# Decoder of two layers: the second layer's chain of the next group woven with the experts of this one

## The reference, cut to what matters

```python
# second layer, x: (16, 100, 256), each part on layernorm(x)
x = x + attn(ln(x))      # q, k, v = bitlinear(h, ternary weights); 16 heads of 16; causal softmax; bitlinear out
x = x + xattn(ln(x))     # q of h (256x256), k and v of the context (128x256), 16 heads, 361 keys, out 256x256
x = x + ffn(ln(x))       # 8 experts and one shared: (gelu(x Wg) * (x Wu)) Wd, weights of the best two of 8

def bitlinear(x, w, g):  # xq: rms norm, then rounded to 8 bits by token; wq: rounded to -1, 0, 1
    return activation_quant(rmsnorm(x, g)) @ weight_quant(w).T
y = einsum('tei,te,eih->th', gelu(g) * u, cw, Wd)    # cw: gate weights, zero for all but two experts
```

## Time and profile before

| | us |
|---|---|
| time, median of 3 runs | 1668.27 (1666.18 to 1669.59) |
| the profiled execution's own time | 1667.32 |
| its span, first to last instruction | 1665.6 |
| PE busy | 1284.8 (77%) |
| DVE busy | 1008.3 (61%) |
| ACT busy | 513.7 |
| POOL busy | 413.2 |
| mean granted clock of PE | 0.861 |

### The profile page before, as it was taken

How to read it: one execution, slowest core, us unless ns; L and a number is a source line. 1 busy time by engine, 2 the same in 40 slices (tenths; PEclk the granted TensorE clock), 3 DMA queues, 4 the chain that set the end, 5 groups by cost and what they waited for, 6 DMA issues and landing times.

```text
span 1665.6 us, 24431 instructions
## 1 busy us (share of the span) xinstructions
PE 1284.8 (77%) x7936; PEld 886.7 (53%) x7936; DVE 1008.3 (61%) x2148; ACT 513.7 (31%) x1269; POOL 413.2 (25%) x528
## 2 busy tenths in 40 slices
PE   2678877878783999952659878689787697986988
PEld 1455644645543566631347654367554575545755
DVE  4457577566563233327668675768657686676852
ACT  2233323324231222201216422246113362233630
POOL 1132234335152100026522112221213212032100
PEclk9688878978896999985769989679898798997998
DMA  9510100390105111111225210144100450104501
GB/s 373 210 47 1 32 16 8 108 382 21 57 18 213 53 45 45 42 39 47 98 45 115 64 40 12 35 90 99 41 12 1 101 122 16 25 11 88 118 7 43
DMA packets 69692, 122.42 MB, mean 73 GB/s; under 512 B 25404, under 2 KB 55100, under 8 KB 68032
## 3 DMA queue, kind: packets, MB, share of 16 engines
q1 hardware_dynamic: 63936, 110.04, 22.0%
q0 software_dynamic: 5632, 10.77, 2.3%
HBM read 67.69 MB, written 53.07 MB: 73 GB/s over the span
## 4 chain that ended last, share of the span: by engine, by line
PE 39%; issue 31%; DVE 10%; POOL 9%; POOLq 3%; DVEq 3%; ACT 2%; DMA 2%; SPq 1%; another core or an unknown queue 0%; ACTq 0%
PE ps L1150 7%; PE ps L1169 3%; PE ps L1323 3%; PE ps L1397 3%; PE ps L1339 3%; PE ps L526 2%; POOL experts L1792 2%; PE ps L1309 2%; PE ps L534 2%; POOL headbd L682 2%; PE ps L1068 1%; PE ps L1046 1%; PE ps L595 1%; PE ps L1410 1%; PE ps L1057 1%
## 5 line engine op out<-in xcount | busy, mean ns | idle before, releaser
L1638 ACT ACTIVATE probs<-ps,small 100x361 f32<-100x361 f32 x256 | 141.5, 558 | 94.9 <-DVE small L2372 89.4
L2372 DVE TENSOR_REDUCE small<-ps 100x2 f32<-100x722 f32 x128 | 115.7, 907 | 37.5 <-PE ps L1309 37.3
L1150 PE MATMUL ps<-every,xT_t 128*128 x256 | 121.7, 599 | 0.4 <-issue 0.4
L1397 PE MATMUL ps<-hT,experts 128*128 128x400 f32 x288 | 115.1, 550 | 1.2 <-DVE small L731 1.2
L1323 PE MATMUL ps<-cst,probs 100*121 100x100 f32 x768 | 104.7, 272 | 7.8 <-DVE probsT L2380 7.4
L1323 PEld LDWEIGHTS ps<-cst,probs 100*121 100x121 f32 x768 | 95.2, 186 | 22.3 <-issue 13.5
L2380 DVE TENSOR_SCALAR probsT<-ps 121x600 f32<-121x600 f32 x128 | 99.2, 775 | 9.8 <-PE ps L1323 9.8
L1339 PE MATMUL ps<-probsT,values_ 121*32 121x100 f32 x1536 | 91.3, 254 | 0.9 <-DVE probsT L2380 0.9
L1309 PE MATMUL ps<-k_stack,q_stack 96*100 96x362 f32 x256 | 82.4, 403 | 6.4 <-ACT probs L1638 5.7
L1199 PE MATMUL ps<-identb,xq 100*128 100x100 bf16 x128 | 13.6, 242 | 88.2 <-DVE y L2247 50.1
L1397 PEld LDWEIGHTS ps<-hT,experts 128*128 128x128 f32 x288 | 59.0, 213 | 41.2 <-issue 12.0
(11 more groups left out here) (328 smaller groups left out, 2896.0 us busy)
## 6 DMA issues: line engine op xcount, KB each, us to landing
k_stack<-key_d SPq DMA_DIRECT2D x192, 90.5 KB, 3.2
tok_d<-wt SPq DMA_DIRECT2D x1, 14848.0 KB, 45.7
res_d<-wt SPq DMA_DIRECT2D x1, 14848.0 KB, 42.8
every<-e_d SPq DMA_DIRECT2D x8, 1536.0 KB, 15.4
ctxT<-ctxT_d SPq DMA_DIRECT2D x8, 726.0 KB, 4.3
key_d<-k_hi SPq DMA_DIRECT2D x32, 181.0 KB, 2.8
key_d<-k_lo SPq DMA_DIRECT2D x32, 181.0 KB, 3.2
gates<-gate_d SPq DMA_DIRECT2D x28, 200.0 KB, 4.4
```

Of the source, the lines that this page charges most:

```text
L1150: ins = e.matmul(ps[:, 2 * i + t % 2, :], xT_t[:, t % 2, c, :], every[:, bass.ds(base + (i * DC + c) * HID0, HID0)], start=(c == 0), stop= ...
L1397: ins = e.matmul(bank(2 * i + j % 2, n=NT), w[:, c, :], hT[:, c, :], start=(c == 0), stop=(c == DC - 1))
L1638: ins = e.activation(f_e[:, n % 2, i, 0:LC], bank(2 * (n % 2) + i, S, LC), ACT.Exp, bias=h_nm[:, n % 2, i:i + 1], accum_out=h_sum[:, b, h: ...
L2372: inc(e.tensor_reduce(h_nm[:, n % 2, 0:2], ps[0:S, 2 * (n % 2):2 * (n % 2) + 2, 0:LC], AX, ALU.max, negate=True), "F_nm")
```

## The change

Self attention of the second layer now takes the code of the first layer's, 16 units of 4 heads. `before_e`, this attention and `after_e` of group g+1 form one chain of 57 steps (18, 21 and 18), and the twelve steps of group g's experts are dealt into it: `dealt` takes an expert step behind the chain's steps 1, 2, 4, 8, 9, 12, 15, 19, 38, 42, 46 and 50. So blocks 0 to 4 and the gate weights lie in `before_e`, block 5 just ahead of the attention, and blocks 6, 7, 8 and the last down and sum in `after_e`.

To have banks for it, the experts use banks 0 to 3 alone: one for gate, one for up (so `gate_up(j)` waits until DVE has read block j-1), two for the sum. `before_e` takes separate banks for its two halves. `after_e` uses one bank for each half. Gate and hidden values and the experts' tokens (`hTG`) lie in weights' space `wt` that is no longer needed. The residual is updated in place in `xall`, and `x_free` is gone. On DVE the first block's product now stands ahead of the gate weights. The loop over groups is unrolled. SP's transfers are the same, but the output of group g is sent from within the feed of group g+1.

```diff
+BEFORE_E, AFTER_E = 9, 9
+GATED_AT = (1, 2, 4, 8, 9, 12, 15, 19, 38, 42, 46, 50)
...
+def both(first, second, rounds):
+    for _ in range(rounds):
+        for st in (first, second):
+            next(st, None)
+            yield
+def dealt(chain, extra, at):
+    for i, _ in enumerate(chain):
+        if i in at:
+            next(extra)
...
@@ PE @@
-            def attend(g, routed):
+            def attend(pre, g, routed=False):
...
             def before_e(g, h):
+                t, o = (6, 4)[h], (7, 5)[h]
...
             def after_e(g, h):
-                yield from toT_pe(e, "E_", g, h, "rTp", b0, xn, ("E_rx", 1))
+                turn_pe(e, "E_", g, h, "rTp", 4 + h, xn, ("E_rx", 1))
+                yield
...
                 if h == 1:
                     e.wait_ge(ld["ctxT3"].sem, g * 16 + 16)
-                    for i in range(3):
-                        kv(g, 0, i)
-                yield
+                    kv(g, 0, 0)
+                yield
+                kv(g, 0, 1 + h)
+                yield
...
+            def inner(g):
+                yield
+                yield
+                yield from attend("E_", g)
+                yield from both(after_e(g, 0), after_e(g, 1), AFTER_E)
+            def chain(g):
+                yield from both(before_e(g, 0), before_e(g, 1), BEFORE_E)
+                yield from inner(g)
...
-            in_turn(late(before_e(0, 1)), before_e(0, 0))
+            in_turn(before_e(0, 0), before_e(0, 1))
+            list(inner(0))
             def group_pe(g, last=False):
-                W(e, "E_kT", g, 1, 1)
-                W(e, "E_v", g, 1, 1)
-                self_pe(e, "E_", g)
-                in_turn(after_e(g, 0), after_e(g, 1))
...
                 if last:
-                    in_turn(experts_g(g))
+                    list(experts_g(g))
                 else:
-                    in_turn(late(before_e(g + 1, 1)), before_e(g + 1, 0), experts_g(g))
+                    dealt(chain(g + 1), experts_g(g), GATED_AT)
+                    W(e, "G_acc", g)
             def experts_g(g):
-                for j in range(E1 + 1):
-                    if j < E1:
-                        if j >= 2:
-                            W(e, "G_hid", g, j - 1)
...
+                def gate_up(j):
+                    if j:
                         W(e, "G_hid", g, j)
+                    for i in range(2):
...
+                            ins = e.matmul(bank(i, n=NT), w[:, c, :], hTG[:, c, :],
+                                           start=(c == 0), stop=(c == DC - 1))
+                    inc(ins, "G_h")
...
+                gate_up(0)
+                yield
+                gate_up(1)
+                yield
+                W(e, "G_top", g)
+                inc(e.transpose(ps[0:NB * 8, 3, 0:S], gates_all[:].rearrange("p b n -> p (b n)"), identS), "G_gTp")
+                down(0)
+                yield
+                yield
+                for j in range(2, E1):
+                    gate_up(j)
+                    down(j - 1)
+                    yield
+                down(E1 - 1)
+                yield
-            with e.Fori(0, NG - 1) as g:
+            for g in range(NG - 1):
                 group_pe(g)
...
@@ DVE @@
             def after_e(g, h):
...
-                if h == 1:
+                e.tensor_scalar(q_isc[:, 2, o], q_isc[:, 2, o], wscale[0:S, 3:4], None, ALU.mult)
+                e.drain()
+                yield
+                if h == 0:
                     value_evac(g, 0, 0)
+                yield
+                if h == 0:
                     value_evac(g, 0, 1)
...
             def experts_g(g):
-                gate_shift_dve(e, NB, g1_shifted, g)
-                e.wait_ge(g1_e.sem, g1_e.at(g))
-                gate_top_dve(e, NB, True, gates_all[:], probs[:, 0, 0:NB * 64], probs[:, 1, 0:NB * 64])
-                e.sem_inc(names["G_top"].sem, 1)
-                for j in range(E1):
...
+                gate_shift_dve(e, NB, g1_shifted, g)
+                hidden(0)
+                yield
+                e.wait_ge(g1_e.sem, g1_e.at(g))
+                gate_top_dve(e, NB, True, gates_all[:], probs[:, 0, 0:NB * 64], probs[:, 1, 0:NB * 64])
+                e.sem_inc(names["G_top"].sem, 1)
+                yield
+                yield
+                for j in range(1, E1):
+                    hidden(j)
                     yield
                 W(e, "G_o", g, E1)
-                inc(e.tensor_tensor(x[:], pair(4), x[:], ALU.add), "G_acc")
+                inc(e.tensor_tensor(group, pair(2), group, ALU.add), "G_acc")
```

460 lines of the change are left out of this document (198 added, 262 removed).

## The result

| | before | after |
|---|---|---|
| time, median | 1668.93 us (1666.18 to 1670.88, 4 runs) | 1715.34 us (1711.14 to 1730.28, 4 runs) |
| span of the profiled execution | 1665.6 | 1728.6 |
| from the second layer's first score to the end | 859.8 | 907.2 |
| PE busy, mean granted clock | 1284.8, 0.861 | 1343.8, 0.847 |

The change is slower by 46.4 us: the ratio is 1.0288, with a 95% interval from 1.023 to 1.0346. The forecast was 1692.

The account below looks back on a forecast made before the run. No engine bounds the whole; Stage A is nearly full on PE, Stage C a chain of latencies with PE half idle. 1667.3 - 17.4 + 20.7 + 21 - 7.7 + 7.6 = 1691.5, forecast 1692 us, range 1668 to 1714.

Parts of the forecast that it names:

- Stage A: Second layer's stretch ahead of the self attention's first score, three times: 54 us each, a gain of 17.4 in all.
- Stage B: Second layer's self attention, four times: 39 us each in units of 4 heads, a cost of 20.7 in all.
- Stage C: From the attention's end to the picks, groups 1 to 3: moved blocks cost 7 us a group, 21 in all.
- The loop: Stage C and D of the looped groups: unrolling removes register work and a branch, 7.7 us less.
- D: From the picks to the experts' first matmul: the added table load of 1.28 us a group counted as 0.
- Stage E: Last group's experts, once: later gate weights, a waiting up of block 2 and the products cost 7.6 us.
- Rival 1: PE is no bound in Stage B and Stage C, which stay at 135 and 34: 1650 us, chance 0.10.
- Rival 2: Stage C runs at 2.4 GHz throughout, 4 us less a group, 12 in all: 1680 us, chance 0.12.
- Rival 3: Units stay slow, with low clock at Stage B's start and Stage A at 57: 1715 us, chance 0.08.

Follow-up runs that it names:

- top_first: Changed kernel with the gate weights computed ahead of the first block's product again, in every group: ratio 1.0303 to the kernel before, second layer 893.0 us.
- one_bank: Unrolled kernel of before with one bank each for gate and up instead of two: ratio 0.9968 to the kernel before, second layer 862.9 us.
- late_c: Changed kernel with blocks 6 and 7 moved behind the turn back: ratio 1.0185 to the kernel before, second layer 879.3 us.
- early_exp: Changed kernel with a one-column exp behind the ninth block's gelu, loading exp's table in Stage C: ratio 1.0145 to the kernel before, second layer 887.0 us.
- fill_d: Changed kernel with eight unread matmuls in PE's pause at D's start, table load left there: ratio 1.0214 to the kernel before, second layer 891.1 us.
- e_banks: Changed kernel with two banks each for gate and up in the last group alone: ratio 1.0202 to the kernel before, second layer 897.4 us.
- fill_more: As unroll_fill, with more unread matmuls in Stage C (32, 16 and 20): ratio 0.9886 to the kernel before, second layer 833.8 us.
- unroll_fill: Unrolled kernel of before with unread matmuls where PE waits in and beside Stage C: ratio 0.9842 to the kernel before, second layer 833.4 us.

## Why the forecast came out too low

The second layer was forecast 24.2 longer and came out 47.4 longer. Of the 23 that are missing, A gives 5.5 and C 4.1, B takes back 6, and 21.5 are the sum for D and the loop: -7.7 forecast, +13.8 measured. By the prediction's own steps:

- **Stage A, forecast 54, measured 55.8.** The bank's waits are real: DVE waits 12.0 and 3.1 for gelu in group 0, against 11.1 in the earlier trace rows, with three blocks fewer. What I left out is PE's own pauses (3.4 for the gate weights, 9.3 for quantised values, in group 0) and the low clock behind them: 0.80 in A instead of 0.93 to 0.95, so that up of block 2 takes 4.44, not 2.92. And the product ahead of the gate weights, which I priced at 2.4, costs 3 (top_first). The single bank, priced at 7 to 8 in each A, costs 4.8 where nothing else is changed (one_bank).
- **Stage B, forecast 39, measured 38.6 and three times 37.1.** The units are 2.19 apart (two in 4.38), as in the earlier trace rows. The tail is 6.3 instead of 7.2 and the first two scores lie 0.85 apart, and in the three groups in which PE comes from dense work the clock is 1.00. The mechanism was right and the term 6 too large.
- **Stage C, forecast +7, measured +8.4 a group.** The turn back is 7.5 later, and "C about 41 to the picks" was met with 41.8. late_c shows that the place makes it: with blocks 6 and 7 behind the turn back the same blocks cost 1.2 a group.
- **The loop, forecast -7.7, measured -18.8.** I had looked for its cost in C and D, by comparing groups, and there unrolling gave 6.6, near my 7.7. The rest I had missed: 8.4 lie at the loop's end, where A turns into B, as two pauses of some 2 us and slower scores behind them. The changed kernel is unrolled too and shows no such pause, but its other costs are larger.
- **D, forecast no cost, measured +13.8, the step that failed.** The words "one before the first maximum is there, so I count 0" were wrong: I counted this load as hidden, but ACT comes to it only behind its last copy of the picks (L1560, done at 1119.73), and from there to the first maximum are 0.96 (early_exp), not 1.28. It makes PE's pause 1.75 instead of 1.4, and the price is the clock: 10 us at half speed, 6.2 a group and 18.6 in all (early_exp); with PE kept busy in that pause the same load costs 0.5 (fill_d). The other load did hide: gelu's at 1075.31 lies under up of block 6. The Trainium skill, ScalarE: Activation LUTs, section "What ACT_TABLE_LOAD costs", adds a drain of 1.38 us; at D's start exp begins at 1121.04, with the end of the load of 1.28 from 1119.75, and no drain stands ahead of the load either, so here the measurement has none. The advice that the prediction took from the same page, all of one set before the next, was the right warning; the price came by way of PE's clock.
- **Stage E, forecast +7.6, measured +7.3, in part by luck.** The second block's pass came 3.3 later as I wrote. But with two banks E is 50.1 with the gate weights as late as ever, and with the gate weights early it is only 1.0 shorter (top_first). The single bank is nearly all of the cost, 6.7 to 6.9 (one_bank, e_banks), where I had put some 4.6 of the 7.6 on it: PE has nothing to do in the wait for the gate weights and comes out of it at the low clock.
- **The rivals.** Rival 1 wanted the turn back within 3 us of the attention's end; it came 9.6 after it. Rival 2 had the clock in C at 4 a group. The projection took 4.6 to 5.0, neither half nor whole, and by fill_more all of C at 2.4 GHz would give at most 2.6. Rival 3's condition, a clock under 0.9 in B, did not occur (0.94 in group 0, 1.00 behind it), yet its time of 1715 was measured: the same sum from other terms.

In steps: 859.8; unrolled 841.0 (-18.8); with single banks 862.9 (+21.9). These two the runs show. The rest are differences of stages between that kernel and the changed one: B, attention in units of 4 heads, +18.3, A -18.7, C +27.2, D +16.6, E +1.0, which makes 907.2 but for roundings. A's -18.7 is what three blocks fewer give less some 9 for the product ahead of the gate weights (top_first). The attention's share was not tried in a kernel of its own; it stands in group 0, which has no experts beside it, as 38.7 against 34.2 in one_bank.

The version that beats both kernels is the unrolled one of before (1652.74 against 1672.54 beside it; the interval of its ratio ends below 1, though it is not clear that it gains 2%). unroll_fill has 1657.88 against 1677.28 beside it; that it is faster than the unrolled one stands in the second layer alone, since the intervals overlap.

## What to carry to other kernels

A moved block costs or gains by its place in the chain, not by its stage: the same blocks cost 8.4 a group with two of them in front of the turn back and 1.2 with all behind it. The banks that such a weave takes from a pipeline can eat most of what it gains: here single banks cost 14.5 in A and 6.7 in E, while A as a whole gained 18.7 against the kernel with single banks. And a short wait of PE has to be priced with the clock behind it: a table load of 1.28, of which 0.3 stuck out, came out at 6.2, a pause of some 2.0 at a loop's branch at some 4.2. Here one tiny activation that loads the table in idle time took the load's cost away.
